# Moving two bias additions of a cross-attention kernel into TensorE and splitting v straight out of PSUM

## What is computed

```python
B, T, E = (8, 2048, 512)          # x comes as (16, 512, 512), ctx as (16, 120, 256)
q = einsum('bte,ef->btf', emb, Wq) + bq
k = einsum('bml,le->bme', latent, Wk) + bk
v = einsum('bml,le->bme', latent, Wv) + bv
w = softmax(einsum('bte,bme->btm', q, k) * E**-0.5, axis=1)   # over t
x = einsum('btm,bme->bte', w, v) + emb
out = (x - mean) * rsqrt(var + 1e-6) * gamma + beta            # mean, var over e
```

## Time and profile before

| | |
|---|---|
| time, median of 3 runs | 264.21 us (263.19 to 264.51) |
| span of the profiled execution, first to last instruction | 263.1 us |
| that execution's time outside the span | not listed; the median run is 1.1 us longer than the span, the shortest 0.1 us |
| busy: DVE / PE / POOL / ACT | 219.9 / 202.3 / 166.0 / 161.6 us |
| mean granted TensorE clock | 0.942 of full speed |

### The profile page before, as it was taken

One profiled execution on the slowest core, in us unless ns is written; L12 is line 12 of the kernel. 1 busy time (PEld: TensorE's weight loads), 2 busy tenths in 40 slices (PEclk: granted clock), 3 DMA queues, 4 the chain that ended last, 5 costly groups with the idle time before them and its releaser, 6 DMA issues.

```text
span 263.1 us, 4154 instructions
## 1 busy us (share of the span) xinstructions
PE 202.3 (77%) x1168; PEld 123.7 (47%) x1168; DVE 219.9 (84%) x436; ACT 161.6 (61%) x343; POOL 166.0 (63%) x164
## 2 busy tenths in 40 slices
...
GB/s 157 291 220 341 351 211 3 1 159 181 159 178 120 204 91 187 85 187 146 159 178 159 178 159 178 140 189 87 202 78 219 90 169 141 0 162 61 100 159 159
DMA packets 11914, 41.04 MB, mean 156 GB/s; under 512 B 1022, under 2 KB 5886, under 8 KB 8062
## 3 DMA queue, kind: packets, MB, share of 16 engines
...
...
## 4 chain that ended last, share of the span: by engine, by line
DVE 34%; ACT 20%; issue 19%; PE 15%; DMA 7%; DVEq 1%; SPq 1%; ACTq 1%; POOL 0%; POOLq 0%
ACT obuf L617 8%; DVE xbuf L836 7%; DMA obuf<-in_ctx 7%; DVE key_junk L764 7%; DVE neg_mean L843 5%; ACT xT L554 4%; PE g_ps L395 4%; DVE s_max L788 3%; DVE stats L848 3%; PE s_ps L425 3%; ACT probs L598 3%; PE pv_ps L417 2%; PE xT_ps L403 2%; ACT ctxT L550 2%; DVE obuf L818 1%
## 5 line engine op out<-in xcount | busy, mean ns | idle before, releaser
L955 POOL TENSOR_TENSOR obuf<-obuf,gamma_all 128x512 f32<-128x512 f32 x44 | 62.3, 1442 | 10.7 <-ACT obuf L617 10.7
L425 PE MATMUL s_ps<-xT,gT 128*120 128x512 f32 x128 | 57.7, 593 | 0.1
L608 ACT ACTIVATE square_junk<-xbuf,neg_mean 128x512 f32<-128x512 f32 x36 | 25.7, 714 | 50.7 <-DVE neg_mean L843 50.4
L403 PE MATMUL xT_ps<-ident,xbuf 128*128 128x128 f32 x256 | 35.8, 284 | 26.3 <-ACT xT L554 25.1
L961 POOL TENSOR_TENSOR obuf<-obuf,beta_all 128x1536 f32<-128x1536 f32 (+1 forms) x16 | 52.3, 3269 | 1.2
L403 PEld LDWEIGHTS xT_ps<-ident,xbuf 128*128 128x128 f32 x256 | 29.5, 144 | 40.7 <-ACT xT L554 30.8
L417 PE MATMUL pv_ps<-v_part,prob_part 120*128 120x512 f16 x135 | 36.5, 389 | 6.5 <-POOL v_part L948 4.1
L843 DVE TENSOR_SCALAR neg_mean<-y_sum 128x2 f32<-128x2 f32 (+1 forms) x20 | 38.3, 1915 | 0.0
L425 PEld LDWEIGHTS s_ps<-xT,gT 128*120 128x120 f32 x128 | 23.2, 183 | 26.2 <-issue 19.0
L554 ACT ACTIVATE xT<-xT_ps 128x512 f32<-128x512 f32 x64 | 34.0, 580 | 1.3 <-PE xT_ps L403 1.3
L617 ACT ACTIVATE obuf<-xbuf,shift,rstd 128x512 f32<-128x512 f32 x44 | 32.5, 799 | 3.4 <-POOL shift L993 3.4
...
## 6 DMA issues: line engine op xcount, KB each, us to landing
...
wv<-in_L_xattn_Wv SPq DMA_DIRECT2D x1, 512.0 KB, 13.9
```

What stands on the lines that cost most here:

```text
L403: mm = pe.transpose(xT_ps[e % 2][:, j, :], xbuf[:, k, j, e * P:(e + 1) * P], ident[:])
L425: mm = pe.matmul(s_ps[0:M, :], gT[:, k % 2, e, :], xT[:, e, :], start=(e == 0), stop=(e == EC - 1))
L955: pool.tensor_tensor(obuf[:, k % 2, j, :], obuf[:, k % 2, j, :], gamma_all[:], ALU.mult)\
```

## The change

u is split into two fp16 parts, transposed by one PE instruction into eight rows (`u_rows`), and added to g by one matmul of 480 columns over an 8-row pattern (`u_spread`), so that g leaves PSUM in one ACT instruction. bv becomes two fp16 rows (`bv_rows`) that one matmul of 512 columns adds to v. Since v is then complete in PSUM, ACT writes HIGH straight from PSUM and DVE writes LOW from PSUM and HIGH; the fp32 copy and POOL's instruction are gone. `v_part` has four places. The bounds take u and bv in.

```diff
 def context_v(b, k):
     pe.wait_ge(ctx_low, b + 1)
     if is_in(b, 1, B):
-        pe.wait_ge(v_copied, b)
+        pe.wait_ge(v_low, b)
...
-    mm.then_inc(v_done, 1)
+    if is_slot(b, 0):
+        pe.wait_ge(bv_rows_done, 1)
+    pe.matmul(v_ps[0:M, :], bv_spread[:], bv_rows[:], start=False, stop=True).then_inc(v_done, 1)
 def context_g(b, k):
     pe.wait_ge(ctx_low, b + 1)
     if is_in(b, 1, B):
-        pe.wait_ge(g_copied, EC * b)
+        pe.wait_ge(g_copied, b)
...
-    mm.then_inc(g_done, 1)
+    if is_slot(b, 0):
+        pe.wait_ge(u_rows_done, 1)
+    pe.matmul(g_ps[:, 0:EC * M], u_rows[:], u_spread[:].rearrange("k e m -> k (e m)"),
+              start=False, stop=True).then_inc(g_done, 1)
 def product(b, k, j):
...
     if j == 2 and is_in(b, 0, B - 2):
-        pe.wait_ge(v_copied, b + 3)
+        pe.wait_ge(v_low, b + 3)
 # PE, before the loop
+            pe.wait_ge(rows_step, 3)
+            pe.wait_ge(w_row_done, 1)
+            pe.transpose(u_ps, u_both[:], ident[:]).then_inc(u_turned, 1)
             context_g(0, 0)
 # ACT
     def copy_g(b, k):
         act.wait_ge(g_done, b + 1)
-        for e in range(EC):
-            act.activation(gT[:, k % 2, e, :], g_v[:, e, :], ACT.Identity, scale=back_g[:],
-                           bias=u_col[:, e:e + 1]).then_inc(g_copied, 1)
+        act.activation(gT[:, k % 2], g_v, ACT.Copy, scale=back_g[:]).then_inc(g_copied, 1)
...
+            act.wait_ge(u_turned, 1)
+            act.activation(u_rows[:], u_ps, ACT.Copy).then_inc(u_rows_done, 1)
             copy_xT(0, 0)
...
-    def v_to_high(b, parity):
-        act.wait_ge(v_copied, b + 1)
-        if is_in(b, 2, B):
-            act.wait_ge(pv_done, RJ * (b - 1))
-        act.activation(v_part[:, parity, HIGH], v_scaled[:, parity], ACT.Copy).then_inc(v_high, 1)
-    if is_in(s, 2, B):
-        v_to_high(s, k % 2)
+    def v_to_high(b, k):
+        act.wait_ge(v_done, b + 1)
+        act.activation(v_part[:, k % RING, HIGH], v_ps[0:M, :], ACT.Copy, scale=onto_v[0:M, :])\
+            .then_inc(v_high, 1)
...
     if is_in(s, 1, B):
+        if is_slot(s, 1):
+            act.wait_ge(onto_done, 1)
+            v_to_high(0, 0)
         exponential(s - 1)
         if is_slot(s, 1):
+            v_to_high(1, 1)
             ctx_to_high(2, 2)
+        elif is_in(s, 2, B - 1):
+            v_to_high(s + 1, k + 1)
         probs_to_high(s - 1)
-    if is_slot(s, 1):
-        v_to_high(0, 0)
...
     if is_slot(s, 1):
-        v_to_high(1, 1)
+        v_to_high(2, 2)
 # DVE, before the loop: after the scales of ctx and QK (over_ctx and u join the bound)
+            rows_next(dve.scalar_tensor_tensor(u_by[:], scale[:, 0:1], 1.0 / ROW_SCALE, scale[:, 1:2],
+                                               ALU.mult, ALU.mult))
+            rows_next(dve.tensor_scalar(u_high[:], u_col[:], u_by[:], None, ALU.mult))
+            dve.tensor_copy(u_both[:, 0:EC], u_high[:])
+            rows_next(dve.scalar_tensor_tensor(u_both[:, EC:2 * EC], u_col[:], u_by[:], u_high[:],
+                                               ALU.mult, ALU.subtract))
 # DVE: after the scales of Wv and v, rows_next waits for each instruction's end
-            dve.tensor_scalar(bv_scaled[:], bv_all[:], scale[:, 3:4], None, ALU.mult)
...
+            rows_next(dve.scalar_tensor_tensor(bv_by[:], scale[:, 0:1], 1.0 / ROW_SCALE, scale[:, 2:3],
+                                               ALU.mult, ALU.mult))
+            rows_next(dve.tensor_scalar(bv_high[:], bv_all[0:2], bv_by[0:2], None, ALU.mult))
+            rows_next(dve.tensor_scalar(bv_taken[:], bv_high[:], ident[0:2, 1:2], -1.0, ALU.mult, ALU.mult))
+            dve.scalar_tensor_tensor(bv_rows[:], bv_all[0:2], bv_by[0:2], bv_taken[:], ALU.mult, ALU.add)\
+                .then_inc(bv_rows_done, 1)
             low_part(wv_part[:, LOW], wv[:], scale[:, 2:3], wv_part[:, HIGH], 3)
...
-    def copy_v(b, k):
-        dve.wait_ge(v_done, b + 1)
-        if is_in(b, 2, B):
-            dve.wait_ge(v_low, b - 1)
-        dve.scalar_tensor_tensor(v_scaled[:, k % 2], v_ps[0:M, :], onto_v[0:M, :], bv_scaled[0:M, :],
-                                 ALU.mult, ALU.add).then_inc(v_copied, 1)
+    def v_to_low(b, k):
+        dve.wait_ge(v_high, b + 1)
+        dve.scalar_tensor_tensor(v_part[:, k % RING, LOW], v_ps[0:M, :], onto_v[0:M, :],
+                                 v_part[:, k % RING, HIGH], ALU.mult, ALU.subtract).then_inc(v_low, 1)
 # POOL
-    if is_in(s, 0, B):
-        pool.wait_ge(v_high, s + 1)
-        pool.tensor_tensor(v_part[:, k % 2, LOW], v_scaled[:, k % 2], v_part[:, k % 2, HIGH],
-                           ALU.subtract).then_inc(v_low, 1)
```

More of the change, by code:

```diff
@@ L394, in context_g @@
                     for n, (c, of_w, of_ctx) in enumerate(steps):
-                        mm = pe.matmul(g_v[:, e, :], qk_part[:, of_w, c, e * P:(e + 1) * P],
-                                       ctxT[:, k % 2, of_ctx, c, :], start=(n == 0), stop=(n == len(steps) - 1))
-                mm.then_inc(g_done, 1)
+                        pe.matmul(g_v[:, e, :], qk_part[:, of_w, c, e * P:(e + 1) * P],
+                                  ctxT[:, k % 2, of_ctx, c, :], start=(e == 0 and n == 0), stop=False)
+                if is_slot(b, 0):
+                    pe.wait_ge(u_rows_done, 1)
+                pe.matmul(g_ps[:, 0:EC * M], u_rows[:], u_spread[:].rearrange("k e m -> k (e m)"),
+                          start=False, stop=True).then_inc(g_done, 1)
             def turn_x(s, k, e):
@@ L502, in slot @@
                 if last:
-                    product(s - 1, k + 1, 3)
+                    product(s - 1, k - 1, 3)
                 if main and not is_slot(s, B - 1):
```

89 lines of the change are left out of this document (62 added, 27 removed).

## The result

The changed kernel takes **273.29 us**, median of 4 runs (270.14 to 274.27). The kernel before, run beside it, takes 264.36 (263.19 to 266.81). The ratio is 1.030 [1.020, 1.039]: slower, by 8.9 us where 6.3 were forecast, and inside the range. The ratio leaves out the slowest of the four executions (274.27 us, 1.5% above the shortest), and that is the profiled one. The interval is 0.9% to either side, or 2.5 us; where less than that matters, rows of the traces are compared, and each trace is a single execution. In every execution listed from here on the launch is 1.8 us longer than its span, so that of the trace before took some 264.9 us (an estimate: 263.1 + 1.8); the prediction had added 1.1.

A forecast was written before the change was run, and what follows sets the result against it. The ring through POOL's beta and `negate` bounds the kernel; 6.2 (start and slot 1) + 0.8 (steady slots) - 0.7 (slot 15) = +6.3 on the 263.1 span gives 269.4, plus 1.1 is 270.5 us; range 266.6 to 273.6.

The forecast's parts named there:

- the ring: Dependency loop setting each slot's 14.18 us: maximum, exponential, HIGH probabilities, first normalisation, POOL's gammas and beta, `negate`, statistics.
- Rivals 2, 3 and 4: Slot 1 costs half, 267.4 us (0.14); ACT's relief shortens slots, 265.9 us (0.07); DVE late for beta, 286 us (0.03).
- Steady slots: Slots 2 to 14: HIGH of v before the probabilities delays `rescale` and gammas, 0.06 a slot, +0.8 us, between 0 and 1.6.
- the slot 4 that I took for an example: Slot where POOL's gamma went ahead of `rescale`; in that order the ring gains 0.08 and loses 0.08, nil.
- my half: Taking half, 0.06 a slot, between `rescale` first (0.12 longer) and gamma first (nil): 0.8 instead of 1.6.
- The bias rows: Added matmuls on PE for v and g, 0.22 us each, together 0.45, hidden under the ring in steady slots.
- The start and slot 1: Everything before slot 2: slot 1 ends 6.2 us later, the start's 1.7 included; slot 2's maximum near 54.7 instead of 48.5.
- the high end of slot 1: 8.5 us later instead of 6.2: longer bv instructions, and PE at the lower clock for some matmuls.
- Sum +1.7: The start: extra DVE steps for bv and u make Wv's LOW part end at 35.5, not 33.8.
- the chain of slot 1: Each v passes PE, ACT, DVE before PE rewrites the bank; v(0) done at 40.6, third product at 49.2 instead of 42.9.
- Behind the slots: Slot 15: without POOL's v instruction the gammas start right behind the first normalisation, -0.7 us, between -0.7 and 0.
- Rival 1: Slots: `key_bias` issued ahead of the second gamma's end, `negate` no longer waits for beta, PE bounds; 243 us, chance 0.06.

The follow-up runs named there:

- the swap: `key_bias` issued ahead of `ctx_to_low` on DVE, nothing else: 240.23 us on the changed kernel, 235.17 us on the kernel before.
- transposes: The changed kernel with 18 extra identity transposes on PE around the transpose of u in the start: 271.51 us.

## Why the prediction was right, and where it was not

**The bound.** Right: the ring through POOL's beta and `negate` sets the slot, before and after. Removing 13.3 us of ACT and 17.9 us of POOL shortened nothing. Rivals 2, 3 and 4 did not happen: slot 1 cost more, not half; the slots grew by 0.107; `key_bias` was not late for beta.

**Steady slots.** +1.3 measured (12 slots), +0.8 forecast (13). The mechanism was right and half its size chosen wrongly: I let `rescale` go first in half the slots. In the changed kernel it went first in all of them, as at 134.36 against 134.39. In the kernel before it had done so in 11 of the 12 slots of the loop, all but the slot 4 that I took for an example, so the half was no reading of the trace. By the rule that the Trainium skill gives (SBUF — State Buffer, Who interferes with whom: an exclusive lock, held by whoever issues first) the term was 1.6; the trace agrees with that rule better than with my half. The experiment with HIGH ahead of the exponential showed the cause, 0.09 a slot of 0.107.

**The bias rows.** Forecast 0.22 each. A row on v lasts 0.42 and lets the next matmul start 0.35 after its own start, a row on g 0.37 and 0.30; at 1.2 GHz they last 0.68 and 0.57. Hidden in the slots, as said, on the chain in slot 1.

**The start and slot 1: the step that failed is the clock of PE's matmuls.** The forecast had slot 2 at 54.7, and it began at 58.90. I had taken a g at 1.42 us and a v at 1.48 throughout, and had named the lower clock only as the high end of slot 1. In the profiled execution the clock was 1.2 GHz from 26.9 to 33.8 and from 44.0 to 47.4: the first g took 2.56, and v(1) with its row 2.83 instead of 1.70.

What my steps cost at the full clock is shown by the changed kernel with the swap. There Wv's LOW part ends at 34.84 (forecast 35.5), v(0)'s at 40.24 (40.6), the third product starts at 49.25 (49.2) and slot 2 at 54.50 (54.7). So "Sum +1.7" and the chain of slot 1 were right in their steps and near in their sizes. Counted from the landing of the context (21.20 in that trace), slot 2 comes 6.6 us later than before there and 11.0 in the profiled execution. The 4.4 between them go with the clock, give or take what the swap does by itself: in the kernel before it brings slot 2 forward by 0.4, so counted.

In pieces: the maximum of slot 1 came 3.7 later, counted from the landing (21.17 against 21.77), and with transposes and the full clock 36.22 - 21.23 = 14.99 behind it, against 13.12 before, which is +1.9. v(0)'s LOW part ended 2.7 later than forecast: 1.5 from Wv's LOW part, the rest because PE came to v(0) only at 38.15, after scores and g(1) that the first g had delayed. From its end to the third product I had 8.6 us (40.6 to 49.2). It took 10.0 (43.29 to 53.30), and 9.0 at the full clock.

Why the clock fell in one execution and not in another stays open. The wait of PE ahead of the first g is not new, and was longer before (1.85 against 1.59).

**Behind the slots.** -2.3 against -0.7. Slot 15 gave 0.4 of the 0.7. Slot 14 gave 0.6, but only because the low clock of the trace before stood in it; without the low clock it takes 9.86 with v as before, so the change made it 0.1 longer, like the others. The remaining 1.3 lie in the last products and normalisations, where the kernel before has the clock at 1.2 GHz from 242.7 to 246.1 and from 249.5 on, and the changed one from 259.1 on. That the clock explains all of it was not tried.

**Luck.** That the time fell inside the range is in part luck. Slot 2 was 4.2 later than forecast and the slots 0.5 longer, and the stretch behind them gave back 1.6 more than forecast, 0.7 of it by the low clock in slot 14 of the trace before.

**Rival 1.** It did not happen by itself, as forecast. But its mechanism is real, larger than anything in the change, and I had only priced it, at 0.06. Its point, `key_bias` issued ahead of the end of the second gamma, held; its time, 243, was close to the 240.2 of the changed kernel with the swap.
